# Second attention of a transformer layer: key and value production moved into the previous head pair's attention, and a tail without its packing copies

## What is computed

```python
x = x + linear_attention(layernorm(x))     # elu+1 feature map
x = x + ffn(layernorm(x))                  # 1024 -> 4096 -> 1024, gelu
x = x + causal_attention(layernorm(x))     # this one is touched by the change
x = x + ffn(layernorm(x))

def causal_attention(x):                   # 16 heads of 64
    q = x @ Wq
    zk = x @ Wk                            # 192 columns
    k = decode(zk, key_decoder)            # per head, complex product
    v = einsum('bsr,hrd->bhsd', x @ Wv, value_decoder)
    q, k = rope(q), rope(k)
    scores = where(causal, q @ k.T / 8, -inf)
    return softmax(scores) @ v @ Wproj
```

## Time and profile before

| | us |
|---|---|
| median of the 2 runs before | 6650.59 |
| their lowest and highest | 6648.63, 6652.55 |
| the profiled execution | 6650.99 |
| its span, slowest core (core 3) | 6649.7 |
| spans of the cores | 6610.2 to 6649.7 |
| PE busy in that span | 4793.2 |
| DVE busy | 1629.0 |
| ACT busy | 1795.7 |

### The profile page before, as it was taken

One profiled execution on the slowest core, in us unless ns is written; L12 is line 12 of the kernel. 1 busy time (PEld: TensorE's weight loads), 2 busy tenths in 40 slices (PEclk: granted clock), 3 DMA queues, 4 the chain that ended last, 5 costly groups with the idle time before them and its releaser, 6 DMA issues.

```text
span 6649.7 us, 56692 instructions; the slowest of 8 cores (6610.2 to 6649.7 us)
## 1 busy us (share of the span) xinstructions
PE 4793.2 (72%) x19408; PEld 1768.1 (27%) x19408; DVE 1629.0 (24%) x2606; ACT 1795.7 (27%) x2350; POOL 81.7 (1%) x158
## 2 busy tenths in 40 slices
PE   3599677749987777557676676676765555997887
PEld 0233222214433333222121121121221112443333
DVE  4444455430002222141303303213122441000000
ACT  2000010103320000005474474564753001331000
POOL 0000000000010000000000000000000000001000
PEclk6799788869998888887786786876877777998998
DMA  3200211132244332200000000000002224226333
GB/s 89 38 1 1 64 51 39 51 76 75 75 110 124 98 101 76 37 1 5 4 5 5 4 5 5 4 5 5 5 5 72 95 89 91 75 75 152 111 105 114
DMA packets 259271, 356.27 MB, mean 54 GB/s; under 512 B 20341, under 2 KB 168053, under 8 KB 256694
## 3 DMA queue, kind: packets, MB, share of 16 engines
q1 hardware_dynamic: 237462, 304.53, 14.1%
q0 software_dynamic: 21536, 48.12, 4.4%
HBM read 257.96 MB, written 142.74 MB: 60 GB/s over the span
## 4 chain that ended last, share of the span: by engine, by line
PE 60%; DVE 15%; ACT 10%; DMA 7%; issue 5%; DVEq 2%; POOL 1%; ACTq 0%; SPq 0%; POOLq 0%
PE f2pyo L580 7%; ACT expb L862 6%; PE f1pyo L580 6%; PE f2pph L533 6%; PE f1pph L533 6%; PE py L826 4%; PE psc L843 4%; PE py L830 3%; DVE xnt L235 2%; PE pr L947 2%; PE ppt L485 2%; PE ppk L313 2%; PE p L679 2%; PE ppv L321 2%; PE pkv L351 2%
## 5 line engine op out<-in xcount | busy, mean ns | idle before, releaser
L862 ACT ACTIVATE expb<-psc 128x1024 bf16<-128x1024 f32 x896 | 894.4, 1023 | 192.2 <-PE psc L850 176.7
L826 PE MATMUL py<-expb,vpair 128*65 128x512 bf16 (+3 forms) x1152 | 476.1, 413 | 405.5 <-ACT expb L862 385.6
L580 PE MATMUL f2pyo<-f2hb,f2w 128*128 128x512 bf16 x2048 | 462.7, 390 | 133.3 <-DMA f2hb<-scr_h 114.2
L580 PE MATMUL f1pyo<-f1hb,f1w 128*128 128x512 bf16 x2048 | 473.0, 395 | 53.0 <-DVE xnt L235 23.7
L533 PE MATMUL f1pph<-xnt,f1w 128*128 128x512 bf16 x2048 | 449.4, 381 | 65.6 <-DMA f1w<-w 60.7
L533 PE MATMUL f2pph<-xnt,f2w 128*128 128x512 bf16 x2048 | 449.4, 381 | 63.9 <-DMA f2w<-w 57.8
L843 PE MATMUL psc<-xnt,kpair 64*128 64x512 bf16 (+3 forms) x1152 | 475.2, 413 | 7.5 <-DVE vpair L778 7.5
L850 PE MATMUL psc<-xnt,kpair 64*128 64x512 bf16 (+3 forms) x1152 | 475.9, 413 | 0.0
L830 PE MATMUL py<-expb,vpair 128*65 128x512 bf16 (+3 forms) x1152 | 473.2, 411 | 0.0
L792 DVE COPY s_tln<-py 1x512 f32<-1x512 f32 x64 | 44.1, 689 | 1536.8 <-PE psc L850 1018.4
L865 ACT ACTIVATE expb<-psc 128x512 bf16<-128x512 f32 (+3 forms) x256 | 112.0, 438 | 841.4 <-PE psc L855 841.4
(11 more groups left out here) (199 smaller groups left out, 4785.2 us busy)
## 6 DMA issues: line engine op xcount, KB each, us to landing
p_xf<-xT SPq DMA_DIRECT2D x16, 2048.0 KB, 8.7
scr_h<-f1hs SPq DMA_DIRECT2D x256, 128.0 KB
f1hb<-scr_h SPq DMA_DIRECT2D x64, 512.0 KB, 10.8
scr_h<-f2hs SPq DMA_DIRECT2D x256, 128.0 KB
f2hb<-scr_h SPq DMA_DIRECT2D x64, 512.0 KB, 8.9
scr<-p_x1f SPq DMA_DIRECT2D x8, 2048.0 KB, 6.9
f1xf<-scr SPq DMA_DIRECT2D x8, 2048.0 KB, 16.7
scr<-f1x2f SPq DMA_DIRECT2D x8, 2048.0 KB, 8.3
```

What stands on the lines that cost most here:

```text
L580: ins = T.matmul(pyo[ot][:, :], w2s[jt][:, ot * 128:ot * 128 + 128], hb[gi][:, jj * 512:jj * 512 + 512], start=(jt == 0), stop=(jt == NJ - 1))
L826: T.matmul(py0[0:65, pcol0:512], vpair[:, pt * 130:pt * 130 + 65], expb[pbank][:, pcol0:512], start=(pt == 0), stop=(pt == plast))
L862: exp_free[bank] = ss.inc(Sc.activation(expb[bank][:, :], psc[bank][:, :], AF.Exp, scale=0.125))
```

## The change

- `kpair` and `vpair` get two buffers each, by the parity of the pair, and the `py` banks 128 partitions instead of 65. `qA` and `qB` go; `rope_q` works in `tB` and in place.
- The production of pair p+1 is cut into pieces that are issued within pair p, behind the py matmuls of a tile: in chunks 0 to 3, at tile 1, two of the eight key chunks each (`prod_kpre2`); in chunk 4, at tile 2, the rotation of pair p+1's queries; in chunk 5, at tile 2, the rotation of its keys (`prod_krope`); in chunks 6 and 7, at tile 1, half of its values each (`prod_vpair`, four groups of four value tiles).
- The pieces use the set of `py` banks that the running chunk doesn't use, and wait for the tail of the chunk before, on DVE and on ACT.
- Value production fills a bank with four tiles before DVE copies them, with two copies for the four.
- Pair 0's keys and values are made by the same functions before its attention; `rope_q(1)` no longer stands there.
- In the tail the copies of the sums are left out. ACT waits for the py matmuls alone and takes the logarithm of each sum straight from PSUM into `r_rstd` and `r_var` (one partition each), then the two exponentials.

The diff, cut to its core:

```diff
@@ rope_q
-                    V.tensor_tensor(qA[:, :], self.xnt[t][:, :], cosr[:, :], ALU.mult)
-                    V.tensor_tensor(qB[:, :], qB[:, :], sinr[:, :], ALU.mult)
+                    V.tensor_tensor(tB[:, :], tB[:, :], sinr[:, :], ALU.mult)
+                    V.tensor_tensor(self.xnt[t][:, :], self.xnt[t][:, :],
+                                    cosr[:, :], ALU.mult)
...
+                def prod_kpre2(pp, kc0, pset):
+                    for i, kc in enumerate((kc0, kc0 + 1)):
+                        cols = slice(kc * 512, kc * 512 + 512)
+                        bank = pys[pset][i]
+                        self.w(T, sv, py_evac[pset])
+                        self.w(T, sv, prod_bank_evt[pset][i])
+                        self.w(T, ss, py_recip[pset])
+                        T.matmul(bank[:, :], b16_0[:, pp * 128:pp * 128 + 128],
+                                 zkt0[:, cols], start=True, stop=False)
+                        e_kp = st.inc(T.matmul(bank[:, :],
+                                               b16_1[0:64, pp * 128:pp * 128 + 128],
+                                               zkt1[0:64, cols],
+                                               start=False, stop=True))
+                        self.w(V, st, e_kp)
+                        ev = sv.inc(V.tensor_copy(kpre[:, cols], bank[:, :]))
...
+                def prod_vpair(pp, g0, ng, pset):
+                    vb = vap[pp % 2]
+                    for gi in range(ng):
+                        g = g0 + gi
+                        bank = pys[pset][gi % 2]
+                        self.w(T, sv, py_evac[pset])
+                        self.w(T, sv, prod_bank_evt[pset][gi % 2])
+                        self.w(T, ss, py_recip[pset])
+                        for s4 in range(4):
+                            stt = g * 4 + s4
...
+                            T.matmul(bank[:, csl], xvt0[:, ssl],
+                                     vdec0[:, pp * 128:pp * 128 + 128],
+                                     start=True, stop=False)
+                            ins = T.matmul(bank[:, csl], xvt1[0:64, ssl],
+                                           vdec1[0:64, pp * 128:pp * 128 + 128],
+                                           start=False, stop=True)
+                        e_vp = st.inc(ins)
+                        self.w(V, st, e_vp)
...
+                        V.tensor_copy(vb[:, g * 4:g * 4 + 4, 0:64],
+                                      srcb[:, :, 0:64])
+                        ev = sv.inc(V.tensor_copy(vb[:, g * 4:g * 4 + 4, 65:129],
+                                                  srcb[:, :, 64:128]))
...
 emit_tail
+                        self.w(Sc, st, e_ylast)
+                        self.w(Sc, self.sh[rb], self.sh[rb].n)
+                        Sc.activation(self.r_rstd[:, :], py0[64:65, :], AF.Ln)
+                        Sc.activation(self.r_var[:, :], py1[64:65, :], AF.Ln)
+                        Sc.drain()
+                        Sc.activation(r_d01[rb][:, 0:512], self.r_rstd[:, :], AF.Exp,
+                                      scale=-1.0)
...
-                        V.tensor_copy(dpak[64:65, :], py0[64:65, :])
-                        e_dp = sv.inc(V.tensor_copy(dpak[96:97, :], py1[64:65, :]))
...
-                        self.w(Sc, sv, py_evac[pyset])
-                        self.w(Sc, self.sh[rb], self.sh[rb].n)
-                        Sc.activation(py0[0:33, :], dpak[64:97, :], AF.Ln)
...
+                        if pp_next is not None:
+                            if t == 1 and c <= 3:
+                                prod_kpre2(pp_next, 2 * c, (c + 1) % 2)
+                            elif t == 2 and c == 4:
+                                rope_evt[pp_next] = rope_q(pp_next)
+                            elif t == 2 and c == 5:
+                                prod_krope(pp_next)
+                            elif t == 1 and c == 6:
+                                prod_vpair(pp_next, 0, 4, (c + 1) % 2)
+                            elif t == 1 and c == 7:
+                                prod_vpair(pp_next, 4, 4, (c + 1) % 2)
```

More of the change, by code:

```diff
@@ L112, in __init__ @@
         self.V.memset(self.ones_c16[:, :], 1.0)
-        self.V.memset(self.tln[:, :], 1.0)
+        self.V.memset(self.tln[:, :], 0.0)
         self.sv.inc(self.V.memset(self.ones_rf[:, :], 1.0))
@@ L741, in attn_b, with prod_krope @@
                 rope_evt[0] = rope_q(0)
[L742 to L753, removed]
-                        self.w(V, st, e_kp)
-                        prod_free[ch % 2] = sv.inc(V.tensor_copy(kpre[:, cols], pk_))
+                def prod_kpre2(pp, kc0, pset):
[11 more added lines that the diff above has]
+                                               start=False, stop=True))
+                        self.w(V, st, e_kp)
+                        ev = sv.inc(V.tensor_copy(kpre[:, cols], bank[:, :]))
+                        prod_bank_evt[pset][i] = ev
+                        pw_evt[pset] = ev
+                def prod_krope(pp):
+                    kb = kpair[pp % 2]
                     V.drain()
@@ L761, in attn_b @@
                     V.drain()
-                    V.tensor_tensor(kpair[:, :], kpre[:, :], cosr[:, :], ALU.mult)
+                    V.tensor_tensor(kb[:, :], kpre[:, :], cosr[:, :], ALU.mult)
                     V.tensor_tensor(tB[:, :], tB[:, :], sinr[:, :], ALU.mult)
                     V.drain()
[L765 to L769, removed]
-                        T.matmul(pv_, xvt0[:, ssl], vdec0[:, p * 128:p * 128 + 128],
-                                 start=True, stop=False)
-                        e_vp = st.inc(T.matmul(pv_, xvt1[0:64, ssl],
-                                               vdec1[0:64, p * 128:p * 128 + 128],
-                                               start=False, stop=True))
-                        self.w(V, st, e_vp)
-                        V.tensor_copy(vap[:, stt:stt + 1, 0:64], pv_[:, 0:64])
-                        prod_free[stt % 2] = sv.inc(
-                            V.tensor_copy(vap[:, stt:stt + 1, 65:129], pv_[:, 64:128]))
@@ L782, in attn_b @@
+                for p in range(8):
+                    pp_next = p + 1 if p + 1 < 8 else None
+                    if p == 0:
+                        for c0 in range(4):
+                            prod_kpre2(0, 2 * c0, (c0 + 1) % 2)
+                        prod_krope(0)
+                        prod_vpair(0, 0, 4, 1)
+                        prod_vpair(0, 4, 4, 0)
+                    self.w(T, sv, vpair_done[p % 2])
+                    self.w(T, sv, kpair_done[p % 2])
                     self.w(T, sv, rope_evt[p])
@@ L786, in emit_tail @@
                         rd_i[0] ^= 1
+                        self.w(Sc, st, e_ylast)
[5 more added lines that the diff above has]
+                                      scale=-1.0)
+                        py_recip[pyset] = ss.inc(
+                            Sc.activation(r_d01[rb][:, 512:1024], self.r_var[:, :],
+                                          AF.Exp, scale=-1.0))
                         self.w(V, st, e_ylast)
-                        self.w(V, ss, dpak_free[0])
                         self.w(V, self.sh[0], self.sh[0].n)
@@ L843, in attn_b @@
                         T.matmul(psc[bank][:, col0:512],
[L844 removed]
+                                 kpair[p % 2][0:64, tsl],
                                  self.xnt[p][0:64, c * 512 + col0:(c + 1) * 512],
```

61 lines of the change are left out of this document (31 added, 30 removed).

## The result

| | before | after |
|---|---|---|
| median, us | 6650.59 | 6280.65 |
| the profiled execution | 6650.99 | 6279.39 |
| slowest core | core 3 | core 4, span 6278.1 |
| ACT busy | 1795.7 | 1826.0 |
| DVE busy | 1629.0 | 1498.9 |

After over before is 0.943, with an interval of 0.941 to 0.945: 5.7% faster. From profile to profile it is 6650.99-6279.39 = 371.6 us, where 318 were forecast.

What follows compares the result with a forecast made beforehand. Between pairs exponentials wait for DVE's rotations; within attention ACT sets the pace at 2.4 GHz, PE at 1.2. Sum 366-4+70+2-45-88+17 = 318 us, 6651-318 = 6333; own range 6260 to 6400 (chance 0.70), eight in ten 6230 to 6440.

Steps and rivals of the forecast that it cites:

- The stretches between pairs: Second attention, seven stretches without exponentials while DVE rotates: they go, hidden inside the previous pair's chunks, 366.2 us gained.
- Rival D: Pair boundaries: a wait makes the next pair's values late again, 125 us on the path, 6458 us; chance 0.02.
- The boundary: Seven pair boundaries: the next pair's first exponential queues on ACT behind the last tail, 0.6 us lost each, 4 us.
- The tails: Chunk ends: ACT returns 1.7 us sooner, less 0.45 for the low clock; net 1.25 for 56 tails, 70 us gained.
- PE comes back 1.7 us earlier into the low-clock stretch: Behind each tail: 1.1 more tiles run at the low clock at 0.41 us extra, 0.45 us lost.
- Key pieces: Key production behind tails in pairs 0 to 6: 1.6 us lost for each of 28, 45 us.
- Value pieces: Value production in chunks 6 and 7 of pairs 0 to 6: 6.3 us lost for each of 14, 88 us.
- The start: Before pair 0's attention: one query rotation gone (11.9 us) and value production shorter (4.8), 17 us gained.
- The last tail: The very last tail of the stage, 4.7 us long before: 2 us gained.
- A, the clock holds: Tails: PE's shorter pause no longer pulls the clock down, 3.0 us gained a tail, 6122 us; chance 0.12.
- B, production at its bounds: DVE's hand-overs pace production: 2.2 us a key piece, 8.4 a value piece, tails gain 0.5; 6421 us; chance 0.12.
- C, the clock down all stage: Second attention: production and tails hold the clock at 0.5 throughout, 6709 us, slower by 0.9%; chance 0.04.

Runs made afterwards that it cites:

- e5: Kernel after, with the four copies of each rotation made twice: first to last tail 1690.4 us, against 1690.1 for the kernel after.
- e6: Kernel after, key and value production moved behind the score matmuls of tile 2, ahead of y of tile 1: 6290.75 us, its slowest core 44 us late beforehand.
- The filler: Score matmuls of tile 2 repeated to keep PE busy in the tail's pause: kernel after 6236.56 and 6240.3 us; kernel before, first to last tail, 1944.7 against 2042.8.
- e3: Kernel after without the 14 pieces of value production inside pairs, so less work than the reference: 6170.8 to 6176.9 us.
- e4: Kernel after without the 28 pieces of key production inside pairs, so less work than the reference: 6230.23 us.
- e8: Kernel after, score matmuls of tile 2 repeated six times in 21 chunks without production on PE: 6236.56 and 6240.3 us; profiled execution 6368.01.
- e12: Kernel before, score matmuls of tile 2 repeated twelve times in all chunks but a pair's first: first to last tail 1944.7 us, against 2042.8 before.

## Why the prediction was right, and where its sum was off

The forecast was 6333 us and the time is 6281, inside the likeliest case's own range and in the direction given. By its items:

1. **The stretches between pairs** (366.2 us) went, and nothing took their place: the longest pause between exponentials is 6.8 us, and `e5` shows that DVE can take four more copies of 1.2 us in each rotation unnoticed. Rival D fell.
2. **The boundary** (forecast 0.6 us lost each). Between the last tail of pair 6 and the first of pair 7, where no key piece stands, lie 9.4 us now. Before there were 50.7, of which 42.2 are the stretch of the earlier trace rows, so 8.5: 0.9 lost each, 6 us in place of 4.
3. **The tails** are the term that was mis-sized: 2.2 us each and not 1.25, 122 to 126 us and not 70. Its direct part was nearly right, 1.89 for 1.7: the four operations took 2.31 us and not 2.45. The failed step is "PE comes back 1.7 us earlier into the low-clock stretch", priced at 0.45 us lost. It took the end of the low stretch as fixed, so that whoever comes back sooner spends longer in it. The traces show PE at 1.2 GHz behind its restart for 4.2 to 4.4 us behind a new tail and 4.6 behind an old one: nothing is lost, and 0.3 us are gained. What decides when the low stretch begins and ends, I did not settle.
4. **Key pieces**: 1.39 us for 1.6, 39 us for 45. The gap on ACT is 1.89 us, 2 had been said.
5. **Value pieces**: 6.8 us for 6.3, 95 for 88. The matmuls ran at 0.22 us, the copies at 0.42, both as priced (the row from which 0.22 was taken gives 0.23). The gap on ACT is 6.77 us, 6 to 7 had been said.
6. **The start**: 17 us were forecast. From the stage's first rotation copy to the first tail's row it was 72.6 us on core 4 and is 52.6 (2942.6 to 3015.2, 2948.5 to 3001.1), 20.0 less and the same on every core; 1.4 of these are the two copies that stood ahead of the row's. So the start gave 18.6. **The last tail**, forecast at 2 us, can't be told: what is left of the 18.9 us lies in stages that the change doesn't touch, and these differ between cores by more.

Measured one by one, the parts between the first and the last tail make 366-6+122-39-95 = 348 of 352.7 us. The rest may be what parts do to each other through the clock: in `e6` pair 7, whose instructions are unchanged, is 1.7 us longer on core 4 than after (188.1 for 186.4).

**The rivals.** A, the clock holds: it didn't, but for the tails it was nearer in kind than the forecast. It wanted 3.0 us a tail, and the new tail with the clock held is worth (201.9-177.4)/7 = 3.5 us against the old one. Of the clock's 1.77 us the shortened pause alone kept about 0.3. The Trainium skill ("TensorE: Matmul & The Clock Gate", section "HAM oscillation") has it that long pauses between bursts of matmuls are what re-throttles the engine, and that the loop is to be rearranged so that PE stays at work. The filler bears out the remedy in this kernel, at 1.77 us a tail; that a pause must be long, the trace does not bear out, since the clock fell at pauses of 2.13 us as at 4.09. B, production at its bounds, fell with `e3` and `e4`, 6.8 and 1.39 us for its 8.4 and 2.2: DVE idles 1.00 us between value groups. C, the clock down all stage, fell with a granted clock of 0.84 over pair 2, production included, where C had 0.5.

The signs named ahead held, but for one: a pair's period is 215 us and not 221 (from the last tail of pair 0 at 3205.3 to that of pair 6 at 4495.4 are six of them). That the clock falls at every tail held, and still the tail was worth more than its price.

## What to carry to other kernels

Where an engine pauses at each step of a loop and its clock falls in the pause, price a tail in two parts, the detour itself and the clock behind it, and don't take the end of the low stretch as fixed. Work that is put into the shade of another engine is best thin, spread over its steps and away from a pause: 32 small matmuls cost 6.8 us in one block behind the tail and 1.7 in 16 units further on. And a bank should be released by the last instruction that reads it, not by the last of its group. Repeating matmuls whose result is written again anyway is a cheap test of what a fallen clock costs, and here it was even a gain.

## What the runs showed of the hardware

- The clock, let fall around each tail, costs 1.77 us behind a pause of 4.1 us on PE, and 1.19 behind one of 2.1, on the average of seven tails. With the pause down to 0.83 us (`e8`) it stayed at 2.4 GHz behind 19 of 21 tails, and with 1.4 to 2.0 us (`e12`) behind all but one of the 48 that are not a pair's first.
- An activation of one partition and 512 columns straight from PSUM takes 0.57 to 0.59 us, no more than one of 33 partitions from SBUF (0.59). The packing copies bought nothing.
- A DVE copy of 128x4x64 from PSUM into strided SBUF takes 0.42 us.
